# Gate of a mixture layer on one Trainium2 core: four one-column fp32 matmuls against two 512-column fp32r matmuls with ones, logits on VectorE

## What is computed

```python
def _dense(x, wi_, wo_):
    return jax.nn.relu(x @ wi_) @ wo_

x = x + einsum('bsd,bdh->bsh', x, W[cat_ids]) + b[cat_ids][:, None, :]      # layer 0
s0 = _dense(x, swi[0], swo[0])                                              # D = 256, F = 1024
s1 = _dense(x, swi[1], swo[1])
eo = relu(einsum('bsd,bdf->bsf', x, wi[type_label])) @ wo[type_label]
gate_in = jnp.concatenate([eo[:, 0], s0[:, 0], s1[:, 0]], axis=-1)          # (2, 768)
w = softmax(relu(gate_in @ g1) @ g2, axis=-1)[:, :, None, None]             # g1 (768, 256), g2 (256, 3)
x = x + eo * w[:, 0] + s0 * w[:, 1] + s1 * w[:, 2]
```

## Time and profile before

| | us |
|---|---|
| median of 3 runs | 271.92 |
| lowest, highest | 271.79, 272.03 |
| the profiled execution, its own time | 271.98 |
| its span in the trace | 270.2 |
| TensorE busy | 264.4 (98%) |
| VectorE, ScalarE, GpSimd busy | 160.2, 148.2, 160.9 |

### The profile page before, as it was taken

The page is one execution under the profiler, slowest core; times in us unless marked ns, Lnnn a source line. Parts: engine busy times, 40 slices in busy tenths (PEclk is TensorE's granted clock), DMA queues, the critical chain, the costliest instruction groups (busy, mean ns, idle before and its releaser), DMA issues.

```text
span 270.2 us, 3474 instructions
## 1 busy us (share of the span) xinstructions
PE 264.4 (98%) x1176; PEld 219.3 (81%) x1176; DVE 160.2 (59%) x239; ACT 148.2 (55%) x257; POOL 160.9 (60%) x170
## 2 busy tenths in 40 slices
PE   8899999999999999999999999999999999999994
PEld 8688888888888888888888888888888888888883
DVE  3779958634654444654445565445566377685683
ACT  2597357665665655665655653645644555545320
POOL 0269989999948949938944724724725628524000
PEclk9999999999999999999999999999999999999999
DMA  6734322022022012102022112112112022000007
GB/s 191 249 106 155 117 78 78 8 74 79 5 75 78 5 74 78 49 33 78 2 78 78 34 46 78 33 45 79 22 58 78 2 78 78 0 0 2 0 21 290
DMA packets 7184, 18.30 MB, mean 68 GB/s; under 512 B 1152, under 2 KB 1664, under 8 KB 7168
## 3 DMA queue, kind: packets, MB, share of 16 engines
q1 hardware_dynamic: 6592, 17.05, 18.9%
q10 hardware_dynamic: 576, 1.05, 1.2%
HBM read 16.00 MB, written 2.10 MB: 67 GB/s over the span
## 4 chain that ended last, share of the span: by engine, by line
PE 96%; DMA 2%; SPq 1%; DVE 0%; ACT 0%; issue 0%
PE acc L638 48%; PE chain L638 23%; PE right L638 12%; PE left L638 7%; PE acc L655 4%; DMA w_raw<-cat_w 2%; PE corner L638 1%; SPq L217 1%; PE left L786 0%; DVE x L533 0%; ACT w_hi L345 0%; PE left L792 0%; SPq L219 0%
## 5 line engine op out<-in xcount | busy, mean ns | idle before, releaser
L257 POOL TENSOR_TENSOR m_lo<-staged,m_hi 128x512 fp32r<-128x512 f32 (+1 forms) x48 | 81.6, 1707 | 80.7 <-ACT m_hi L333 65.7
L638 PE MATMUL acc<-h_hi,m_lo 128*128 128x512 f32 x192 | 74.7, 389 | 0.0
L638 PE MATMUL acc<-h_lo,m_hi 128*128 128x512 f32 x192 | 74.7, 389 | 0.0
L638 PE MATMUL acc<-h_hi,m_hi 128*128 128x512 f32 x192 | 74.7, 389 | 0.0
L357 ACT COPY kept<-chain 128x512 f32<-128x512 f32 x66 | 38.8, 588 | 57.8 <-PE chain L638 57.8
L638 PEld LDWEIGHTS acc<-h_hi,m_hi 128*128 128x128 f32 x192 | 36.0, 188 | 7.5
L638 PEld LDWEIGHTS acc<-h_hi,m_lo 128*128 128x128 f32 x192 | 36.0, 188 | 7.5
L638 PEld LDWEIGHTS acc<-h_lo,m_hi 128*128 128x128 f32 x192 | 36.0, 188 | 7.5
L460 DVE SCALAR_TENSOR_TENSOR h_lo<-left,h_hi 128x512 fp32r<-128x512 f32 x24 | 16.6, 692 | 29.9 <-ACT h_hi L369 29.9
L257 POOL TENSOR_TENSOR staged<-staged 128x128 f32<-128x128 f32 x66 | 30.9, 483 | 1.7
L465 DVE TENSOR_TENSOR left<-left,kept 128x512 f32<-128x512 f32 x22 | 15.3, 697 | 26.7 <-PE left L638 26.7
(11 more groups left out here) (93 smaller groups left out, 435.0 us busy)
## 6 DMA issues: line engine op xcount, KB each, us to landing
staged<-mlp_w SPq DMA_DIRECT2D x22, 512.0 KB, 3.3
x<-x_t ACTq DMA_DIRECT2D x4, 256.0 KB, 4.1
staged<-mlp_w SPq DMA_DIRECT2D x4, 256.0 KB, 3.5
x<-x_t SPq DMA_DIRECT2D x4, 256.0 KB, 5.7
out_t<-x SPq DMA_DIRECT2D x2, 512.0 KB, 3.3
out_t<-x SPq DMA_DIRECT2D x4, 256.0 KB, 2.8
g_sb<-g SPq DMA_DIRECT2D x1, 768.0 KB, 3.7
w_raw<-cat_w SPq DMA_DIRECT2D x4, 128.0 KB, 3.3
```

Source lines behind the costliest of these rows:

```text
L257: return nc.gpsimd.tensor_tensor(out, a, b, ALU.subtract)
L638: last = nc.tensor.matmul(out[:], half[:, slot, at:at + P], moving, start=(start and n == 0), stop=(stop and n == 2), skip_group_check=True)
```

## The change

The partial sums no longer serve as weights but as the moving operand. `gate_part` (128 x 512, both batch rows) is split into `gate_hi` (ACT copy, at the end of its group 17) and `gate_lo` (DVE subtraction, at the end of its group 17); both lie where `t_raw` lies. In group 18 two fp32r matmuls with ones as weights put the 512 sums in every partition of `left`. DVE then makes six instructions of 256 elements (relu and product with a row of g2, which lies in all partitions, 3 x 256), writes them over `g1_sb`, and one reduction of 1,536 elements gives the six logits in SBUF. The matmul of group 19 goes; product 2 of group 19 waits for the six instructions; product 2 of group 20 has no wait of its own any more. g2 is broadcast to the partitions on the host. Tensors behind `g2_sb` in SBUF move, and the filler grows from 40 to 64.

```diff
-PAD = 40
+PAD = 64
@@
+        with ExitStack() as late:
+            gate_hi = sb("gate_hi", [P, B * D], F32R, late)
+            gate_lo = sb("gate_lo", [P, B * D], F32R, late)
         t_raw = sb("t_raw", [P, 4, TOK])
@@
-        g2_sb = sb("g2_sb", [P, DC, 3])
+        g2_sb = sb("g2_sb", [P, 3, D])
-        ones = sb("ones", [P, P])
+        ones = sb("ones", [P, P], F32R)
-        gate_h = sb("gate_h", [P, B * DC])
-        logit_half = sb("logit_half", [P, B, 3])
-        logit_part = sb("logit_part", [P, B, 3])
+        logits = sb("logits", [P, B, 3])
@@ ACT, after the other work of group j
+                if j == KEPT * GROUPS + 1:
+                    act.wait_ge(gate_sums, 12)
+                    nc.scalar.copy(gate_hi[:], gate_part[:].rearrange("p b n -> p (b n)")).then_inc(gate_hi_ready, 1)
                 if j == 4 * GROUPS + 3:
                     act.wait_ge(logits_done, 1)
                     act.wait_ge(neg_max_ready, 1)
                     for b in range(B):
-                        nc.scalar.activation(exps[:, b, :], left[:, 8 + b * 3:11 + b * 3], ACT.Exp, bias=neg_max[:, b:b + 1],
+                        nc.scalar.activation(exps[:, b, :], logits[:, b, :], ACT.Exp, bias=neg_max[:, b:b + 1],
@@ DVE, gate_logits
+                terms = g1_sb[:].rearrange("p (k b) n -> p k b n", b=B)
                 dve.wait_ge(gate_hidden_done, 1)
-                nc.vector.tensor_scalar(gate_h[:], left[:, 0:B * DC], 0.0, None, ALU.max).then_inc(gate_steps, 1)
-                dve.wait_ge(gate_steps, 1)
-                for b in range(B):
-                    nc.vector.tensor_scalar(logit_half[:, b, :], g2_sb[:, 0, :], gate_h[:, b * DC:b * DC + 1], None,
-                                            ALU.mult).then_inc(gate_steps, 1)
-                for b in range(B):
-                    dve.wait_ge(gate_steps, b + 2)
-                    nc.vector.scalar_tensor_tensor(out=logit_part[:, b, :], in0=g2_sb[:, 1, :],
-                                                   scalar=gate_h[:, b * DC + 1:b * DC + 2], in1=logit_half[:, b, :],
-                                                   op0=ALU.mult, op1=ALU.add).then_inc(gate_steps, 1)
+                for k in range(3):
+                    for b in range(B):
+                        nc.vector.scalar_tensor_tensor(out=terms[:, k, b, :], in0=left[:, b * D:(b + 1) * D], scalar=0.0,
+                                                       in1=g2_sb[:, k, :], op0=ALU.max, op1=ALU.mult).then_inc(gate_terms, 1)
+                dve.wait_ge(gate_terms, 3 * B)
+                nc.vector.tensor_reduce(logits[:].rearrange("p b k -> p k b"), terms, AX.X, ALU.add).then_inc(logits_done, 1)
@@ DVE, after the other work of group j
+                if j == KEPT * GROUPS + 1:
+                    dve.wait_ge(gate_hi_ready, 1)
+                    subtract(gate_lo[:], gate_part[:].rearrange("p b n -> p (b n)"), gate_hi[:].bitcast(F32)).then_inc(gate_split, 1)
                 if j == KEPT * GROUPS + 2:
                     gate_logits()
@@ PE, product 2
                     if j == KEPT * GROUPS + 3:
-                        pe.wait_ge(gate_steps, 1)
-                    if j == KEPT * GROUPS + 4:
-                        pe.wait_ge(neg_max_ready, 1)
-                        pe.wait_ge(exps_ready, B)
+                        pe.wait_ge(gate_terms, 3 * B)
@@ PE, in the loop, ahead of product 4
                 if j == KEPT * GROUPS + 2:
                     pe.wait_ge(h_split, 4 * j + NTH[0])
-                    pe.wait_ge(gate_sums, 12)
-                    for b in range(B):
-                        for d in range(DC):
-                            last = nc.tensor.matmul(left[:, b * DC + d:b * DC + d + 1], gate_part[:, b, d * P:(d + 1) * P],
-                                                    ones[:, 0:1], start=True, stop=True)
-                    last.then_inc(gate_hidden_done, 1)
-                if j == KEPT * GROUPS + 3:
-                    pe.wait_ge(h_split, 4 * j + NTH[0])
-                    pe.wait_ge(gate_steps, 1 + 2 * B)
-                    nc.tensor.matmul(left[:, 8:8 + B * 3], ones[:], logit_part[:].rearrange("p b k -> p (b k)"),
-                                     start=True, stop=True).then_inc(logits_done, 1)
+                    pe.wait_ge(gate_split, 1)
+                    nc.tensor.matmul(left[:], ones[:], gate_hi[:], start=True, stop=False)
+                    nc.tensor.matmul(left[:], ones[:], gate_lo[:], start=False, stop=True).then_inc(gate_hidden_done, 1)
@@ host
-        "g2": feature_major(L1_cond_g2, 0),
+        "g2": np.broadcast_to(np.asarray(L1_cond_g2).T, (P, 3, D)),
```

More of the change, by code:

```diff
@@ L146, in build @@
         gate_sums = sem("gate_sums")
+        gate_hi_ready = sem("gate_hi_ready")
+        gate_split = sem("gate_split")
         gate_hidden_done = sem("gate_hidden_done")
-        gate_steps = sem("gate_steps")
+        gate_terms = sem("gate_terms")
         logits_done = sem("logits_done")
@@ L380, in _ @@
             act.wait_ge(ones_ready, 1)
-            nc.scalar.activation(table[:], ones[:, 0:1], ACT.Relu)
+            nc.scalar.activation(table[:], ones[:, 0:1].bitcast(F32), ACT.Relu)
             load_x(act, 0, 1)
@@ L491, in gate_logits @@
             def gate_logits():
+                terms = g1_sb[:].rearrange("p (k b) n -> p k b n", b=B)
                 dve.wait_ge(gate_hidden_done, 1)
-                nc.vector.tensor_scalar(gate_h[:], left[:, 0:B * DC], 0.0, None, ALU.max).then_inc(gate_steps, 1)
-                dve.wait_ge(gate_steps, 1)
-                for b in range(B):
-                    nc.vector.tensor_scalar(logit_half[:, b, :], g2_sb[:, 0, :], gate_h[:, b * DC:b * DC + 1], None,
-                                            ALU.mult).then_inc(gate_steps, 1)
-                for b in range(B):
-                    dve.wait_ge(gate_steps, b + 2)
-                    nc.vector.scalar_tensor_tensor(out=logit_part[:, b, :], in0=g2_sb[:, 1, :],
-                                                   scalar=gate_h[:, b * DC + 1:b * DC + 2], in1=logit_half[:, b, :],
-                                                   op0=ALU.mult, op1=ALU.add).then_inc(gate_steps, 1)
+                for k in range(3):
[4 more added lines that the diff above has]
+                nc.vector.tensor_reduce(logits[:].rearrange("p b k -> p k b"), terms, AX.X, ALU.add).then_inc(logits_done, 1)
             def gate_max():
                 dve.wait_ge(logits_done, 1)
-                nc.vector.tensor_reduce(neg_max[:], left[:, 8:8 + B * 3].rearrange("p (b k) -> p b k", b=B), AX.X, ALU.max,
+                nc.vector.tensor_reduce(neg_max[:], logits[:], AX.X, ALU.max,
                                         negate=True).then_inc(neg_max_ready, 1)
@@ L544, in x_lo_of @@
                 subtract(x_part(x_lo, b, t, d), x1_part(b, t, d), x_part(x_hi, b, t, d).bitcast(F32)).then_inc(x_split[b][t], 1)
-            nc.vector.memset(ones[:], 1.0).then_inc(ones_ready, 1)
+            nc.vector.memset(ones[:].bitcast(F32), 1.0).then_inc(ones_ready, 1)
             for d in range(DC):
@@ L756, in _ @@
             for _ in range(WARMUP):
-                nc.tensor.matmul(left[:, 0:P], ones[:], ones[:], start=True, stop=True)
+                nc.tensor.matmul(left[:, 0:P], ones[:].bitcast(F32), ones[:].bitcast(F32), start=True, stop=True)
             def layer0_of(b):
```

## The result

| | before | after |
|---|---|---|
| median of the runs, us | 271.87 (6 runs) | 273.98 (6 runs) |
| lowest, highest | 271.67, 272.03 | 273.48, 274.07 |
| profiled execution: time, span | 271.98, 270.2 | 273.48, 271.3 |
| median of time less span | 1.79 | 2.22 |

The changed kernel is slower: ratio 1.0074, 95% interval 1.0064 to 1.0084, 2.1 us on the medians; the forecast was 273.6 us. The span runs from the first to the last instruction of the trace, and "time less span" is the device time that lies outside it; before's 1.79 comes from its executions beside the experiments. The profiled execution is the shortest of its six.

A forecast was written before the change was run, and what follows sets the result against it. The prediction took TensorE, 96% of the chain at 2.4 GHz, to bound the kernel. From 271.98 us it subtracted 0.72 saved and added stalls of 1.16 and 1.15, giving 273.6 us, range 272.4 to 274.3.

The forecast's parts named there:

- TensorE's savings: Groups 18 and 19: two matmuls replace the gate's four, 0.45 us saved; the logits matmul goes, 0.27 us; together 0.72 us.
- Hold 1: Product 6 of group 18: TensorE stalls 1.16 us for ScalarE's `kept`, queued behind the new gate copy.
- Hold 2: Product 2 of group 19: TensorE stalls 1.15 us until VectorE's six term instructions have read `left`.
- The full drain: Six terms in group 19 without overlap: 2.5 us, a second stall of 1.6 us and 274.0 us; the trace spoke against it.
- Covered work: Groups 18 and 19: `gate_lo` subtraction 0.69 us, reduction about 1.75 us, g2's load some 2 us more, all taken as hidden.
- The sum: Whole kernel: profiled 271.98 us less savings of 0.72, plus stalls of 1.16 and 1.15, gives 273.6 us, 0.6% slower.
- rival C: VectorE dearer: terms 0.42 to 0.48 us each without overlap, or reduction slowed beside GpSimd; 274.0 to 274.4 us; chance 0.15.
- rival D: Group 18: the two new matmuls run as two records each, adding 0.45 us, 274.0 us; chance 0.02.
- A: Groups 18 and 19: TensorE is held only once, 272.4 us, within 0.2% of before; chance 0.10.
- B: Groups 18 and 19: no stall, only the removed work shows, 271.26 us, faster; chance 0.07.
- priced at nothing: Maximum, exponentials and mixing stay and only their input moves to SBUF; no cost was put down.
- E: Two stalls of 1.2 us could cost TensorE's 2.4 GHz clock grant; 275 us or more; chance 0.02.

The follow-up runs named there:

- kernels without holds: Two versions of both edits: VectorE's reduction cut in two and moved to its waits, 271.33 us; six terms also summing, no reduction, 271.32 us.
- the late copy: Changed kernel with ScalarE's gate copy moved behind the activation of `left` in group 18, VectorE's `gate_lo` subtraction moved along: 272.75 us.
- both edits: Changed kernel with the late copy, and `left` read once by one VectorE instruction of 512 columns, which alone releases product 2 of group 19: 274.69 us.
- the idle fill: The late copy with one more VectorE instruction, a fill of 512 columns nobody reads, ahead of the maximum in group 19: 274.74 us.

## Why the prediction was right, point by point

- **TensorE's savings.** 0.45 us was put down for the new pair, 0.46 measured; the matmul of group 19 is gone. The kernels without holds show the saving whole: their median spans are 269.4 and 269.45 against 270.1, 0.65 to 0.7 less, where the sum had 0.72.
- **Hold 1.** Predicted 1.16, measured 1.09. The copy started 0.04 us after the twelfth sum (199.80 to 199.84), not 0.09. The copy, the pitch of 0.52 and TensorE's lag (0.22 for 0.23) came as read from group 3. That ScalarE's wait and copy are enough, without VectorE's wait, is shown by the copy alone in the kernel before.
- **Hold 2.** Predicted 1.15, measured 1.06. The six terms took 2.07 us against 2.12, and the release 0.17 against 0.2. Interpolating the duration between 4 and 512 columns, and taking the overlap from the row of 208.51, was right within 3%. The full drain between them, which the prediction weighs against the row, would have made 2.5 us; the six started 0.33 us apart. The section that it quotes (the Trainium skill, "VectorE: DVE Perf Modes", "The DRAIN you can't avoid") itself adds that a next operation that is not held starts earlier, so the page and the row do not contradict each other as the prediction has it.
- **Covered work.** The subtraction took 0.69 us and the reduction 1.75, both as put down. `left` of group 19 ended at 213.80 and ScalarE read it at 214.35: 0.55 us to spare, against 0.5. g2's 384 KB landed in 4.9 us and SP's next load went out at 34.20 instead of 33.96, which is 0.73 us later counted from the issue of g1 (29.41 and 29.90), where 2 us had been allowed; TensorE shows no hold behind it.
- **The sum.** From the first layer-0 matmul to the end of TensorE's chain the trace has 258.76 us before (7.81 to 266.57) and 260.35 after (7.30 to 267.65): 1.59 us, the sum that was forecast. That the two agree to the hundredth is luck. Hold by hold it is 1.09 + 1.06 - 0.72 = 1.43; most of the other 0.16 (0.13 within groups 18 and 19) is a slightly wider pace (0.23 to 0.24 us) behind each hold, which had not been foreseen and made up for the two holds being read a little large.
- **What was missed.** Time less span was taken to stay at 1.8 us and rose by 0.4. It makes 274.0 out of 273.6, and was no term of the sum. The same 274.0 stands in the prediction three times, as the lower end of rival C, for rival D and for the drain; that it was measured speaks for none of them, since the trace shows none of their terms.
- **The rivals.** A (one hold) and B (none) are out for this kernel; A is what the late copy measures, where 272.4 was put down and 272.75 came, 0.4 of it again outside the span. C's prices did not come: the terms lay 0.33 us apart and the reduction took 1.75. C named GpSimd as the danger, for the reduction. The right neighbour, the wrong instruction: the edge lies in group 20 at `x<-y`, where the kernel before had 0.21 us in hand and the changed one 0.13 (second start 223.42, `m_lo` at 223.55). The difference was priced at nothing: the exponentials read the logits from SBUF and take 0.30 and 0.28 us instead of 0.26 and 0.25, and `x<-y` starts 1.54 us behind the maximum instead of 1.47. The change came within 0.13 us of costing 2 us more. The prediction looked for holds only up to `left` of group 19. D is out: each new matmul is one record.
- **The clock**, E: it stayed up behind holds of 1.1 us; it fell behind one of 2.1 us in the profiled execution of both edits, and not behind one of 2.3 us in that of the idle fill.
- **Wording.** Where the prediction speaks of "a second" between two starts, a microsecond is meant.

## What to carry to other kernels

An engine's in-order queue makes a small instruction expensive when it waits: before you put one in, find what is queued behind it and who waits for that, and release a PSUM bank with one early read instead of with the last of a series. Here the early read alone made the kernel slower; it paid only once VectorE's work behind it was shortened or moved. Where VectorE and GpSimd both work on SBUF, note by how much each pair of them misses the other; a few tenths of VectorE time upstream can turn the order and cost the length of the other's instruction. Once the edge is known, the same edit can be made to pay: here undoing the two holds and moving the reduction into idle time were worth 2.65 us between them, of which 2.35 us lie in the span. The margin of 0.13 us stayed as thin as it was.

## What was not expected of the hardware

- Order decides: 1.28 us for `x<-y` if it starts 0.13 us before GpSimd's `m_lo`, 3.15 us if it starts 0.12 us after it. A fill of 0.48 us was enough to turn one into the other.
- Summing a written result of 256 columns added almost nothing to the pace of VectorE (0.35 us from start to start with it, 0.34 without), with a read of 0.08 us beside the next instruction.
- Time less span moves by 0.2 to 0.4 us, up or down, when a single idle VectorE instruction is put in.
